# A fused attention and feed-forward block on one core: the rotary pair as one operation, heads interleaved over partitions, another order of the opening

## The reference

```python
x = x + tanh(g_xattn[0]) * xattn(layernorm(x), ctx, mask, rms_scale, q_w, kv_w, out_w)
x = x + tanh(g_ffn[0])   * ffn(layernorm(x), W1, b1, W2, b2)
# xattn: 4 heads of 64 share one key/value head
xn, mn = rmsnorm(x, rms_scale), rmsnorm(mem, rms_scale)
q = rope(einsum('BTD,NDH->BTNH', xn, q_w), S + t) * 64 ** -0.5
k, v = rope(mn @ k_w, s), mn @ v_w
p = softmax(where(mask, q @ k.T, MASK_FILL))
return einsum('BTNH,NHD->BTD', p @ v, out_w)
# rope: [x1 * cos - x2 * sin, x2 * cos + x1 * sin], halves of 32
# ffn: gelu(x @ ternary(W1).T + b1) @ ternary(W2).T + b2
```

## Time and profile before

| | us |
|---|---|
| median of 3 timed runs (lowest, highest) | 308.92 (308.06, 309.13) |
| the profiled execution | 309.19 |
| its span, first to last instruction | 307.4 |
| PE busy | 295.4 |
| DVE busy | 243.2 |
| ACT busy | 234.3 |
| POOL busy | 131.1 |

### The profile page before, as it was taken

The page is one execution under the profiler, slowest core; times in us unless marked ns, Lnnn a source line. Parts: engine busy times, 40 slices in busy tenths (PEclk is TensorE's granted clock), DMA queues, the critical chain, the costliest instruction groups (busy, mean ns, idle before and its releaser), DMA issues.

```text
span 307.4 us, 6780 instructions
## 1 busy us (share of the span) xinstructions
PE 295.4 (96%) x2119; PEld 274.6 (89%) x2119; DVE 243.2 (79%) x819; ACT 234.3 (76%) x601; POOL 131.1 (43%) x152
## 2 busy tenths in 40 slices
PE   5996999989999999999999999999999999999996
PEld 5975999878999899989998899989998999889886
DVE  2589899999987889779886899878977897567443
ACT  2596787898697967897588959796788958883581
POOL 8376878692246305522334414630542333511300
PEclk9999899999999999999999999999999999999999
DMA  6970000200202002100201010100210000100202
GB/s 204 286 243 2 0 3 0 71 0 2 69 3 68 2 0 70 53 17 2 68 13 55 0 54 15 51 17 0 71 52 17 2 0 11 61 3 0 70 0 68
DMA packets 12281, 13.27 MB, mean 43 GB/s; under 512 B 823, under 2 KB 11696, under 8 KB 12256
## 3 DMA queue, kind: packets, MB, share of 16 engines
q1 hardware_dynamic: 11452, 12.29, 12.6%
q10 hardware_dynamic: 708, 0.46, 0.5%
q0 software_dynamic: 96, 0.21, 0.4%
HBM read 8.76 MB, written 4.19 MB: 42 GB/s over the span
## 4 chain that ended last, share of the span: by engine, by line
PE 85%; DVE 7%; issue 2%; ACT 2%; DMA 1%; POOL 0%; ACTq 0%; DVEq 0%
PE ps_m L1293 22%; PE ps_h L1293 22%; PE ps_m L1526 17%; PE ps_s L1293 9%; PE ps_t L1301 4%; PE ps_t L1471 4%; PE ps_t L1447 2%; DMA gate_row<-in_gates 1%; PE ps_t L1546 1%; PE ps_m L1546 1%; DVE s_neg L1025 1%; PE ps_t L1479 1%; DVE pT_lo L938 1%; ACT hT_hi L699 1%; ACT h_all L699 1%
## 5 line engine op out<-in xcount | busy, mean ns | idle before, releaser
L487 POOL TENSOR_TENSOR prob<-prob,p_inv 128x512 f32<-128x512 f32 x32 | 34.2, 1069 | 66.8 <-DVE p_inv L1041 66.7
L1086 DVE TENSOR_TENSOR hT_lo<-h_all,hT_hi 128x512 fp32r<-128x512 f32 x64 | 42.2, 686 | 18.6 <-ACT hT_hi L699 18.6
L1293 PE MATMUL ps_h<-x1nT_hi,w_tern 128*128 128x512 f32 x128 | 54.4, 425 | 1.2 <-ACT hT_hi L699 0.9
L1526 PE MATMUL ps_m<-w_tern,hT_hi 128*128 128x256 f32 x224 | 55.2, 287 | 0.0
L1526 PE MATMUL ps_m<-w_tern,hT_lo 128*128 128x256 f32 x224 | 53.6, 279 | 0.0
L665 ACT ACTIVATE prob<-s_neg,s_min 128x154 f32<-128x154 f32 x128 | 52.4, 416 | 1.2 <-DVE s_min L1036 1.1
L699 ACT ACTIVATE h_all<-ps_h,b_sb 128x512 f32<-128x512 f32 x64 | 44.6, 697 | 8.2 <-PE ps_h L1293 7.0
L1293 PE MATMUL ps_h<-x1nT_lo,w_tern 128*128 128x512 f32 x128 | 50.6, 395 | 0.0
L463 POOL TENSOR_TENSOR q_cos<-q_cos,q_sin 128x256 f32<-128x256 f32 x32 | 23.6, 738 | 58.4 <-DVE q_sin L992 57.6
L1293 PE MATMUL ps_m<-vw_hi,pT_hi 128*128 128x256 f32 (+1 forms) x160 | 45.5, 284 | 0.0
L1293 PE MATMUL ps_m<-vw_hi,pT_lo 128*128 128x256 f32 (+1 forms) x160 | 44.8, 280 | 0.0
(11 more groups left out here) (162 smaller groups left out, 778.2 us busy)
## 6 DMA issues: line engine op xcount, KB each, us to landing
x_sb<-in_x SPq DMA_DIRECT2D x8, 512.0 KB, 3.5
out_x<-x_both SPq DMA_DIRECT2D x8, 384.0 KB, 2.5
h_all<-in_w1t SPq DMA_DIRECT2D x1, 1024.0 KB, 11.1
w_raw<-in_w2t SPq DMA_DIRECT2D x1, 1024.0 KB, 13.4
out_x<-x_both SPq DMA_DIRECT2D x8, 128.0 KB, 1.7
x_both<-in_ctx_main SPq DMA_DIRECT2D x1, 512.0 KB
wo_raw<-in_wo SPq DMA_DIRECT2D x2, 256.0 KB, 8.4
x_both<-in_wq ACTq DMA_DIRECT2D x1, 256.0 KB, 6.5
```

The lines of the kernel that those rows point to most:

```text
L487: pool.tensor_tensor(main, main, inv.to_broadcast([P, H, P]), ALU.mult)
L1086: dve.tensor_tensor(hT_lo[:, c, :], h_act[c % 4][:], hT_hi[:, c, :], ALU.subtract).then_inc(h_split, 1)
L1293: m = pe.matmul(dst, lhs, rhs, start=(n == 0), stop=(n == len(pairs) - 1))
L1526: m = pe.matmul(dst, a[:, c, P * t:P * (t + 1)], w[:, c, :], start=(c == 0 and a is hT_hi), stop=(c == NF - 1 and a is hT_lo))
```

## The change

It has six parts.

1. The query rotation is one DVE operation of 128x512 (`q_both` = the projected tile, read twice, times cos and sin), where there were two of 128x256. The columns of a query tile are ordered (c h), heads innermost, so that after `q_T` two heads share the 128 partitions alternately, and not as halves. The keys stand in all 128 rows twice and are masked by `parity` (a column of 0 and 1 each): `kk_rounded` and `kk_rest` have a scale now. The tables `rq` are joined from the loaded ones by two POOL copies (`join_tables`).
2. The mean is taken out of the query weights by a product with a centring matrix (`scale_centre` on ACT, `centre_wq` on PE, four products of 128x256) in place of `sum_wq` and two DVE operations. `wq_rest` reads PSUM.
3. `keep_warm` streams 512 columns of zeros and not 128 of ones: four such products at the start (behind POOL's fill of `prob_tail`), one more before the context's transposes; the others are gone. `k_products` also streams the value weights, so 128 columns and not 64 (the upper half is overwritten and never read).
4. `x_sb[1]` is loaded before the query tables. Its transposes of group 0 go to `x1nT`, so those of group 1 needn't wait. Two of the four context tails are loaded by ACT's queue, and `gate_row` last there.
5. `vw_rest` of products 3, 4, 6 and 7 is done by POOL (`VW_ON_POOL`), out of a second copy that ACT writes. POOL's fills of `kk_hi` and `kk_lo` are gone.
6. Every `fill()` has another order. The loop's order is the same.

```diff
@@ blocks of the program @@
-        VW_ON_POOL = ()
+        VW_ON_POOL = (3, 4, 6, 7)
...
+        def x_tiles(i):
+            return (x1nT_hi, x1nT_lo) if isinstance(i, int) and i == 0 else (xT_hi, xT_lo)
...
             sp.dma_start(rk_sin[:], rope_k_sin).then_inc(tab_in, 16)
+            sp.dma_start(x_sb[1][:], x_g[1]).then_inc(x_in[1], 16)
...
+            def join_tables():
+                pool.wait_ge(rope_in, 32)
+                pool.tensor_copy(rq[:, :, 0].rearrange("p t (j c) -> p t j c", j=2),
+                                 rq_cos.rearrange("p t (o c) -> p t o c", o=1).to_broadcast(
+                                     [P, 2 * NT, 2, C // 2])).then_inc(rope_set, 1)
+                pool.tensor_copy(rq[:, :, 1], rq_sin).then_inc(rope_set, 1)
...
             def mask_biases():
+                pool.wait_ge(centre_set, KD)
...
-                q = q_cos[t % 2][:].rearrange("p (h j c) -> p h j c", h=H, j=2)
-                swapped = q_sin[t % 2][:].rearrange("p (h j c) -> p h j c", h=H, j=2)[:, :, ::-1, :]
-                pool.tensor_tensor(q, q, swapped, ALU.add).then_inc(q_roped, 1)
+                cos, sin = (q[t % 2].rearrange("p (j n) -> p j n", j=2) for q in (q_cos, q_sin))
+                pool.tensor_tensor(cos, cos, sin[:, ::-1, :], ALU.add).then_inc(q_roped, 1)
...
+                for j in range(2):
+                    for dst, src in kk_parts(kk_hi, S * j):
+                        nc.scalar.activation(dst, src, ACT.Copy, scale=parity[:, j:j + 1]).then_inc(kk_hi_set, 1)
...
-                cos = rq_cos[:, pos, :].rearrange("p (a c) -> p a c", a=1).to_broadcast([P, 2 * H, C // 2])
-                dve.scalar_tensor_tensor(q_cos[t % 2][:].rearrange("p (a c) -> p a c", a=2 * H),
-                                         q.rearrange("p (a c) -> p a c", a=2 * H), r, cos, ALU.mult, ALU.mult)
-                sin = rq_sin[:, pos].rearrange("p (a j) c -> p a (j c)", a=1).to_broadcast([P, H, C])
-                dve.scalar_tensor_tensor(q_sin[t % 2][:].rearrange("p (h c) -> p h c", h=H),
-                                         q.rearrange("p (h c) -> p h c", h=H), r, sin,
+                tables = rq[:, pos].rearrange("p a (c o) -> p a c o", o=1).to_broadcast([P, 2, C, H])
+                twice = q.rearrange("p (o c h) -> p o c h", o=1, h=H).to_broadcast([P, 2, C, H])
+                dve.scalar_tensor_tensor(q_both[t % 2][:].rearrange("p a (c h) -> p a c h", h=H), twice, r, tables,
                                          ALU.mult, ALU.mult).then_inc(m_read, 1)
...
-            def keep_warm(n, dst=ps_h[1]):
+            def keep_warm(n):
+                pe.wait_ge(zeros_set, 1)
+                zeros = prob_tail[:].rearrange("p t h s -> p (t h s)")
                 for _ in range(n):
-                    pe.matmul(dst[:, 0:P], ones_sb[:], ones_sb[:], start=True, stop=True)
+                    pe.matmul(ps_h[1][:], ones_sb[:], zeros, start=True, stop=True)
...
-                    m = products(ps_h[1][:, C * t:C * (t + 1)],
-                                 [(ctx_T[k][:, P * t:P * (t + 1)] if t < B else ctx_T_tail[k], wkv[:, 0, k, :])
+                    m = products(ps_h[1][:, C * t:C * (t + 2)],
+                                 [(ctx_T[k][:, P * t:P * (t + 1)] if t < B else ctx_T_tail[k], wkv[:, :, k, :])
                                   for k in range(KD)])
...
+            def centre_wq():
+                pe.wait_ge(centre_set, KD)
+                pe.wait_ge(wq_in, 16)
+                for k in range(KD):
+                    m = products(ps_m[0][:, H * C * k:H * C * (k + 1)],
+                                 [(centre[:, j, P * k:P * (k + 1)], wq_raw[:, j].rearrange("p (a g c) -> p c g a", a=HP, g=2)) for j in range(KD)])
```

More of the change, by code:

```diff
@@ L1593, in fill @@
-                q(SECOND, 2)
                 q(SECOND, 3)
-                tail_T(FIRST, 0)
+                q_T(SECOND, 1)
+                scores(SECOND, 0)
+                vw_product(5)
                 tail_T(FIRST, 1)
-                vw_product(5)
-                scores(SECOND, 0)
-                q_T(SECOND, 1)
-                vw_product(6)
                 p_T(FIRST, 1)
                 attend(FIRST, 0)
+                vw_product(6)
+                q_T(SECOND, 2)
+                scores(SECOND, 1)
@@ L1630, in fill @@
                 ffn_in(SECOND, 0)
-                tail_T(SECOND, 2)
                 ffn_in(SECOND, 1)
```

439 lines of the change are left out of this document (234 added, 205 removed), and 6 rows, old and new, of the table FILL_T.

## The result

| | median us | ratio to before, 95% interval |
|---|---|---|
| before (14 runs) | 308.63 | |
| changed (14 runs) | 309.88 | 1.0045 [1.0026, 1.0064] |

A forecast was written before the change was run, and what follows sets the result against it. TensorE was taken as the bound (295.4 of 307.4 us busy), waiting for VectorE early on. Terms +0.4 - 1.8 + 0.5 - 1.1 = -2.0 on the profiled 309.19 gave 307.2 us, 8-in-10 range 305.4 to 309.6.

The forecast's parts named there:

- That the loop was untouched: From 80 to 290 us: order unchanged, PE busy 208.87 of 210 us, so VectorE's savings there count as nothing.
- First term: First 20 us, up to the first query rotation: rotation 0.4 us later, bounds 0 and 0.9.
- a first rotation behind 22: Sign of being wrong, in the opening; the right sign was a first rotation at 20.0 to 20.9 us.
- Centring: Opening, on PE: four products of 256 columns, 0.43 us each, taken as nothing; uncovered at most 1.7 us.
- The late `wo`: Opening: `wo` lands 1.9 us later behind `x_sb[1]`; `wo_rounded` ends near 19 us on ACT, ahead of the values.
- Second term: From the first rotation to the first scores: work leaving VectorE's order makes the stretch 1.8 us shorter.
- Third term: Behind the first scores: new PE waits of 0.3, 0.2 and 1.2 us less 1.24 of old idle, +0.5 us.
- Fourth term: Low clock from 30.06 to 33.47 us mostly goes: 1.1 us gained, bounds 0 and 1.7.
- the first rival: Low clock stretch comes back elsewhere, after PE waits near 19 to 23 us; fourth term 0, 308.3 us; chance 0.20.
- POOL: Third rival: POOL becomes the bound from 30 to 60 us, needing 32.7 us; 309.9 us; chance 0.10.
- the late `x_sb[1]`: Fourth rival: its load arrives late for the sums near 15.5 us; 310.7 us if at 19; chance 0.05.
- The second rival: Opening's copies and wide products hidden, low stretch gone whole (-1.7), 0.2 spared in the third term: 305.7 us; chance 0.15.

The follow-up runs named there:

- two_operations: Changed kernel with the query rotation as two VectorE operations of 128x512's halves (128x256) again, same layout; ratio to before 1.0054.
- parity_last: Changed kernel with `parity` allocated behind all other tensors, so what lay behind it moves back by 32 bytes; ratio to before 0.9999.
- before_pads: Kernel before with two unused tensors added, so later tensors lie 1024 and then 1056 bytes further on, as after the change; ratio to before 1.0018.
- queries_apart: Changed kernel with POOL writing the rotated query sums to their own buffer, so query transposes load 128 adjacent columns; ratio to before 1.0025.
- centre_rows: Changed kernel with `centre_wq` streaming the raw query weights in stored order, ACT and VectorE reordering as they read PSUM; ratio to before 1.0030.
- hidden_aligned: Changed kernel with an unused 8 bytes a partition (32 padded) ahead of `w2_tern`, putting it and `hT` at multiples of 64 bytes; ratio to before 1.0051.
- narrow_warm: Changed kernel with `keep_warm` as five products of 128 columns of ones in place of five of 512 columns of zeros; ratio to before 1.0105.
- mended: Changed kernel with the edits of centre_rows_wo_behind, parity_last and queries_apart together; ratio to before 0.9960.
- centre_rows_wo_behind: centre_rows with ACT's `wo_rounded` moved behind `v_rounded(0)` and `kk_rounded`, and POOL's `wo_rest` behind the first two tiles' rotated sums; ratio to before 1.0013.

## Why the prediction was wrong

The profiled execution was forecast 2.0 us sooner and came 1.5 later. Of these 3.5 us, 2.0 were missed in the opening and 1.33 in the loop; 0.14 lie behind the loop. Without the loop's part the change would have been worth nothing, with the opening as forecast it would still have been faster: so both failed, and each by a step of its own.

**That the loop was untouched: wrong.** "From 80 to 290 us PE is busy 208.87 of 210 us ...; the order there is unchanged, so what VectorE saves there lies beside PE's work and counts as nothing." The part on VectorE is right (two_operations), and TensorE is still 99.5% busy, 208.95 us. What failed is the step behind it, "Edits at nothing: the strided inputs of the transposes ...", and the silence on the memory map. With TensorE 99.5% busy, some ns on many of its instructions were paid nearly in full: 1.1 us by the starts of the 448 products, 1.02 of the loop in parity_last. The map costs 0.9 to 1.0 us (before_pads, parity_last), the stride 0.5 (queries_apart), together somewhat more than the 1.33 of the loop. That a stride costs nothing was an estimate without a row under it, and both strides cost: the centring's streamed query weights step by 64 and 128 floats, and 0.90 us became 0.45 without the step (centre_rows); the query transposes load every second float, and their 198 ns became 139 (queries_apart).

**First term, +0.4, was +2.8 (22.77 less 19.97).** This is a sign of being wrong that the prediction had named, "a first rotation behind 22". The step that failed is "Centring: four products of 256 columns ... Taken as nothing; uncovered it would be at most 1.7." They stand in the chain to `v_products`, so they were uncovered, and they took 3.58 and not 1.7. The late `wo` was named too ("`wo_rounded` then ends near 19 on ACT, ahead of the values") and mis-sized: it ended at 20.54. In this execution that held nothing up, since `v_products` came later still. It does where the centring is shortened, or where the transfer lands late, at 20.0 to 20.7 (centre_rows, parity_last, two_operations, hidden_aligned): the rotation of parity_last starts at 23.59. So taking away the stride alone uncovered `wo`. The four wide products ended at 7.95 and not 6.9 (1.53 us each, between the bounds of 0.86 and 1.72: their rows of 512 columns, two a product, start 0.85 us apart from 2.82 to 6.23 and 0.43 apart from 6.99), and the keys began 0.83 later. With both mends the rotation starts at 21.20, still 1.2 later than before; how much of that rest is the wide products' was not tried apart.

**Second term, -1.8: right.** From the rotation to the release of the second scores are 6.88 us (22.77 to 29.65), before 9.53: 2.65 less, where 2.66 was summed from rows. `vw_product(0)` behind it took 0.60 (30.58 to 31.18), not 0.86, so the term was -2.05.

**Third term, +0.5, was +1.1.** Idle time from 30 to 80 us is 2.33 against 1.24. The wait ahead of `ffn_in(SECOND, 2)` is 1.32 (1.2 forecast), at 68.62; the 0.93 at 46.52 for `pT_lo` was not seen.

**Fourth term, -1.1: the low stretch is absent, its worth unmeasured, at most -1.7.** The stretch of the earlier trace rows does not appear in the changed kernel, nor in narrow_warm, so the wide products aren't what keeps the level there. What does is open. A wait of 1.31 us stood ahead of it before, and in centre_rows the clock fell within a wait of 1.91 us, as the first rival had it; but in mended and centre_rows_wo_behind TensorE waits 1.50 and 1.42 us ahead of the first scores, and the granted clock stays at 1.00. The length of one wait doesn't decide it. And 1.7 us may be far too much: five executions of the kernel before had a mean granted clock of 1.00, so no such stretch, and took under 311 us; their median is 308.27, that of the 79 others under 311 us 308.57. That is 0.3 us, of five executions. VectorE's 3.35 busy us in the 3.41 of that stretch would explain it.

The four as measured are +2.8, -2.05, +1.1 and up to -1.7: +0.15, where the mark has moved by 0.03. That they agree rests on taking the fourth at its bound. With it the opening, forecast at -2.0, lost 2.4 us by the first term and 0.6 by the third and won 0.85 in the others; if the fourth is worth less, some other gain was overlooked, and no run shows which. The loop adds 1.33. Neither of the rivals on the slow side, POOL or the late `x_sb[1]`, took place: POOL is at 27.92, and `x_sb[1]` was not waited for in the changed kernel. It came close: VectorE waited for it 0.48 us in parity_last, 0.49 in two_operations and 1.04 in centre_rows. The second rival's 305.7 is 0.3 lower than its own terms give (307.2 - 0.4 - 0.6 - 0.2 = 306.0); nothing rests on it.

## What to carry to other kernels

An edit that adds or lengthens a tensor can move the later ones: the tables and `parity` moved `hT_hi` by 1056 bytes here. Where TensorE is the bound, compare its groups' mean durations before and after for lines that the diff does not touch; a few ns on 448 products were here most of the loss that was measured. Allocate small additions last, or compare the tensors' places mod 128 bytes before and after. Price an operand's stride as an unknown with a factor of two, as the centring's was (0.90 us against 0.45), above all if the operation stands in a chain, and when one of two causes is removed without effect, remove both before dropping the theory.
